# Evacuations of attention projections on VectorE, and the pair projections one head earlier

## The reference

```python
# x: (8, 2048, 1024); layer 0: latent attention, causal, 16 heads, clip, 64 + 32 rope columns
c_q = x @ W_DQ;  Qc = c_q @ W_UQ;  Qr = rope(c_q @ W_QR)
c_kv = x @ W_DKV; Kc = c_kv @ W_UK; Kr = rope(x @ W_KR); V = c_kv @ W_UV
attn = softmax(where(causal, clip(Q @ K.T, -80, 80), -inf) / sqrt(96)) @ V
# layer 1: plain attention, 16 heads of 64, no mask used
q = (x @ q_w.T + q_b) / 8;  k = x @ k_w.T + k_b;  v = x @ v_w.T + v_b
attn = softmax(q @ k.T) @ v
# each block: x = x + layernorm(block(layernorm(x)))
```

## Time and profile before

| What | us |
|---|---|
| Median of 2 runs | 5481.67 (5463.56 and 5499.78) |
| Profiled run | 5459.5 |
| Its span, slowest core | 5457.9 |
| Spans of the eight cores | 5430.5 to 5457.9 |
| PE busy | 3475.7 (64%) |
| DVE busy | 1663.3 (30%) |
| ACT busy | 1806.0 (33%) |

### The profile page before, as it was taken

How to read it: one execution, slowest core, us unless ns; L and a number is a source line. 1 busy time by engine, 2 the same in 40 slices (tenths; PEclk the granted TensorE clock), 3 DMA queues, 4 the chain that set the end, 5 groups by cost and what they waited for, 6 DMA issues and landing times.

```text
span 5457.9 us, 48911 instructions; the slowest of 8 cores (5430.5 to 5457.9 us)
## 1 busy us (share of the span) xinstructions
PE 3475.7 (64%) x10539; PEld 1024.8 (19%) x10539; DVE 1663.3 (30%) x2197; ACT 1806.0 (33%) x2222; POOL 194.1 (4%) x272
## 2 busy tenths in 40 slices
PE   2566666665446666656687687777775466566664
PEld 1111111111112222221111111111111112121211
DVE  3344445455722433321111211211214624010101
ACT  2144444442233221134444444444442320212120
POOL 0000000000000011100000000000000000000000
PEclk9666666666668888875555555555556698989897
DMA  3000000001047332231101101001000056121213
GB/s 77 13 5 5 4 5 4 4 5 19 1 138 219 103 103 93 85 78 31 29 0 29 27 2 29 20 10 29 8 18 18 27 163 197 54 70 54 70 54 116
DMA packets 132278, 275.24 MB, mean 50 GB/s; under 512 B 25731, under 2 KB 60979, under 8 KB 132022
## 3 DMA queue, kind: packets, MB, share of 16 engines
q0 software_dynamic: 62208, 154.22, 10.5%
q10 hardware_dynamic: 45840, 75.51, 4.1%
q1 hardware_dynamic: 23974, 42.38, 2.6%
HBM read 237.02 MB, written 41.94 MB: 51 GB/s over the span
## 4 chain that ended last, share of the span: by engine, by line
PE 45%; DVE 19%; DMA 13%; ACT 11%; issue 10%; DVEq 1%; ACTq 1%; POOLq 0%; SPq 0%; POOL 0%
PE psB L511 11%; PE ps_up L1000 8%; PE psA L461 7%; DVE rrow L523 7%; PE psB L531 4%; ACT pbuf L480 4%; PE ps_dn L1023 3%; PE psB L461 3%; PE ps_dn L1623 2%; DMA w2q_scr<-w2b 2%; DMA w2b<-w2q_scr 2%; DMA wdnq_scr<-w2b 2%; DMA w2b<-wdnq_scr 2%; ACT sqd L1620 2%; ACT hbuf L1610 1%
## 5 line engine op out<-in xcount | busy, mean ns | idle before, releaser
L511 PE MATMUL psB<-pbuf,v_km 128*65 128x512 bf16 (+3 forms) x1664 | 787.6, 564 | 254.1 <-ACT pbuf L480 165.1
L523 DVE RECIPROCAL rrow<-psB 1x512 f32<-1x512 f32 x128 | 429.0, 3352 | 1182.6 <-PE psB L511 1179.4
L480 ACT ACTIVATE pbuf<-psA,negb 128x1024 bf16<-128x1024 f32 x368 | 408.5, 1114 | 445.9 <-PE psB L511 350.9
L1023 PE MATMUL ps_dn<-w2b,hbuf 128*128 128x512 bf16 x1536 | 400.8, 400 | 131.8 <-DMA w2b<-w2q_scr 35.5
L531 PE MATMUL psB<-rrow,c_ones_f 1*64 1x512 f32 x256 | 221.5, 962 | 319.7 <-DVE rrow L523 311.3
L461 PE MATMUL psA<-qpair,kpair 64*128 64x512 bf16 x736 | 375.9, 617 | 28.0 <-ACT pbuf L480 24.3
L480 ACT ACTIVATE pbuf<-psA,nb 128x1024 bf16<-128x1024 f32 (+7 forms) x288 | 255.1, 895 | 357.8 <-PE psB L511 263.4
L1000 PE MATMUL ps_up<-xqT,w1b 128*128 128x512 bf16 x1024 | 250.6, 409 | 171.8 <-DVE hscr L1159 91.5
L511 PEld LDWEIGHTS psB<-pbuf,v_km 128*65 128x65 bf16 x1664 | 170.5, 141 | 835.9 <-issue 832.0
L1623 PE MATMUL ps_dn<-sqd,c_ones_cf 128*1 128x512 f32 x256 | 134.3, 606 | 296.4 <-ACT sqd L1620 296.4
L1000 PE MATMUL ps_up<-xnT,w1b 128*128 128x512 bf16 x1024 | 258.8, 398 | 28.7 <-DVE w1b L1058 21.5
(11 more groups left out here) (257 smaller groups left out, 3462.7 us busy)
## 6 DMA issues: line engine op xcount, KB each, us to landing
w1b<-w1q_scr POOLq DMA_DIRECT2D x24, 1024.0 KB, 6.5
w2b<-w2q_scr POOLq DMA_DIRECT2D x48, 512.0 KB, 4.0
w1b<-wupq_scr POOLq DMA_DIRECT2D x24, 1024.0 KB, 5.8
w2b<-wdnq_scr POOLq DMA_DIRECT2D x48, 512.0 KB, 3.9
al_wf<-wupt ACTq DMA_DIRECT2D x64, 256.0 KB, 2.8
al_wf<-wdnt ACTq DMA_DIRECT2D x64, 256.0 KB, 2.9
xs<-x SPq DMA_DIRECT2D x1, 8192.0 KB
wqf<-w1t SPq DMA_DIRECT2D x8, 1024.0 KB
```

Of the source, the lines that this page charges most:

```text
L480: P.op("scalar", lambda e, sc_ap=sc_ap, pb=pb, kw=kw: e.activation(pb, sc_ap, AF.Exp, **kw), reads=pres, sreads=sr, writes=(pbres,))
L511: q_start=q_start, lastkc=lastkc: e.matmul(psB[:, gq:gq + nn][0:65, :], v_km[:, kc * (H * 65) + h * 65: kc * (H * 65) + h * 65 + 65], pb[: ...
L523: P.op("vector", lambda e, b=b: e.reciprocal(rrow[:], psB[64:65, b * 512:(b + 1) * 512]), reads=(bres,), writes=("rrow",))
L1023: hx=hx, dnp=dnp: e.matmul(dnp[:, n2 * 512:(n2 + 1) * 512], hbuf[:, hc * 512 + qc * 128: hc * 512 + qc * 128 + 128], w2band[bs][:, hx * D ...
```

## The change

Four edits. In layer 0 the six projection evacuations of a head become a `tensor_copy` on DVE. In layer 1 the four evacuations of a pair become a `tensor_scalar` on DVE (multiply, then add the bias), and the two squares of the bounds a `tensor_tensor` on DVE. And the items for pair j+1 ride on the first head of pair j instead of the second, with the bounds directly behind that head. The alpha pieces and the weight loads stay ahead of each pair.

```diff
             def post(slot, half=half):
                 pst, sbase, pres = slot
-                P.op("scalar", lambda e, pst=pst, sbase=sbase, half=half:
-                     e.activation(dst_fn(half),
-                                  pst[:, sbase:sbase + 1024][0:rows, :],
-                                  AF.Identity),
+                P.op("vector", lambda e, pst=pst, sbase=sbase, half=half:
+                     e.tensor_copy(dst_fn(half),
+                                   pst[:, sbase:sbase + 1024][0:rows, :]),
                      reads=pres, writes=(dres,))
...
-                P.op("scalar", lambda e, pst=pst, sbase=sbase, half=half:
-                     e.activation(dst[:, half * 1024:(half + 1) * 1024],
-                                  pst[:, sbase:sbase + 1024], AF.Identity,
-                                  scale=sc, bias=bias[:, j:j + 1]),
+                P.op("vector", lambda e, pst=pst, sbase=sbase, half=half:
+                     e.tensor_scalar(dst[:, half * 1024:(half + 1) * 1024],
+                                     pst[:, sbase:sbase + 1024], sc,
+                                     bias[:, j:j + 1], ALU.mult, ALU.add),
                      reads=pres, sreads=(bres,), writes=(dres,))
...
-            P.op("scalar", lambda e, srcp=srcp:
-                 e.activation(bsq[:], srcp[:], AF.Square),
+            P.op("vector", lambda e, srcp=srcp:
+                 e.tensor_tensor(bsq[:], srcp[:], srcp[:], ALU.mult),
                  reads=(sres,), writes=BSQR)
...
-            extra = pair_prod_items(j + 1) if (hh == 1 and j + 1 < 8) else ()
+            extra = pair_prod_items(j + 1) if (hh == 0 and j + 1 < 8) else ()
             emit_attention_head(
...
-        if j + 1 < 8:
-            pair_bounds(j + 1)
+            if hh == 0 and j + 1 < 8:
+                pair_bounds(j + 1)
```

## The result

| | us |
|---|---|
| Before, median of 10 runs | 5489.3 |
| After, median of 12 runs | 5553.1 |
| Ratio | 1.0112, 95% interval 1.0075 to 1.0150 |
| Profiled runs, span of the slowest core | 5457.9 before, 5532.5 after |

What follows compares the result with a forecast made beforehand. DVE's chain was taken to bound layer-0 head ends; in layer 1, ACT's alpha pieces and the bounds chain counted. 112 + 3 - 24.5 + 18 = 108.5, say 109 us, on 5474 gave 5583 us (+1.99%), range 5530 to 5640.

Steps and rivals of the forecast that it cites:

- the forecast's own +85 to +130: Whole kernel, main case: slower by +85 to +130 us, chance 0.66.
- the first rival: Layer-0 head ends hide more of the evacuations: +40 to +85 us, about 5535; chance 0.12.
- DVE's chain in layer 0: Layer-0 head ends: evacuations in DVE's queue delay the next scores by 7.5 us, 15 x 7.5 = 112 us.
- its own sign of being wrong: The forecast called itself wrong if, among other signs, the layer-0 ends grow by under 6 us.
- The second miss: Layer-0 head end, first broadcast matmul behind 3.4 us of idle PE: taken at 1.93 us, not 1.04.
- The +3 for the projections ahead of the first heads: The 8 + 4 projections ahead of the first heads are serial too: +3 us, bounds 0 to 5.
- The hidden evacuation: Layer-0 head end: last evacuation, behind the last rope step, hidden by the DMA; without that cover it costs 1.2 us.
- Layer 1: Layer-1 head ends: -24.5 us from both ends, +18 from pair loads, gain 6.5 us; bounds -37 to +22.
- Long end: Layer-1 head end with projections and bounds, last exp to next exp: 52.6 us before, 38.4 forecast.
- short end: Layer-1 head end without projections, now with the alpha pieces: 14.5 us before, 25.2 forecast, +3 where pair loads fall.
- The price of the pair loads: Layer-1 short ends: pair loads among the alpha pieces cost +3 us in six ends, +18; bounds 0 and 7 an end.
- The clock's rival: Layer-1 heads keep TensorE's 2.4 GHz level behind the long end: sum -31 us, 5443; chance 0.04.

Runs made afterwards that it cites:

- the kernel with the early loads: Layer 0 of before, layer 1 of after, weight loads of a pair emitted one head earlier; 0.9969 (0.9956 to 0.9981) against the kernel before.
- the run with layer 0 alone: Kernel before with only the six projection evacuations of a layer-0 head on DVE; 1.0136 (1.0113 to 1.0160), 74 us.
- With the loads moved away: Layer 0 of before, layer 1 of after, weight loads two pairs ahead behind a POOL wait on negb; 0.9943 (0.9922 to 0.9965) against before.

## Why the prediction was right or wrong

It gave 5583 us, 109 above its base of 5474, and the range 5530 to 5640. The measured medians are 64 us apart, the ratio says 61, and 5553 lies in the range. That is in part luck. The difference of 61 us does not lie in the forecast's own +85 to +130, which had 0.66, but in the case of the first rival, +40 to +85, which had 0.12; and the measured median of before is 15 us above the base. Within 2% had 0.46, and slower by over 2%, which did not happen, 0.51. The order of the queues and the waits came as told. Two durations taken from one head end were too long, and one effect was not in the sum.

*DVE's chain in layer 0 (+7.5 a head, 112 us): right in kind, nearly a quarter too large.* Measured are 6.1 us a head on the slowest cores, 5.9 on the mean of all, and 90.8 us for the stage. That is at the edge of its own sign of being wrong, under 6 us. By its steps, on the slowest cores: the first reciprocal was to start 4.1 us late, it was 3.4 (3.1 over all cores); between the reciprocals 0.95 was forecast, 0.56 measured; behind them 2.5 and 2.24.

The largest miss is the first. The head that I had read had a slow second projection (1.89 us, 488.52), and the sum took that for every head. In before it takes over 1.6 us in 48 of the 120 head ends of all cores, in after in 11; on the slowest core of after it takes 1.04 to 1.22 us in 11 of 15. Since the reciprocal now stands behind it, it starts that much sooner. This could have been read from the other head ends of before.

The second miss could not. It is the step "After 3.4 us of idle PE I take it at the duration of the one behind 2.9 us of idleness": of 15 first broadcasts ten took 1.04 to 1.2 us and five 1.8 to 1.94, all behind 3.0 to 3.8 us of idle PE; over all cores 57 of 120 were slow. In before all 120 first broadcasts, behind at most 1.2 us of idle PE, were fast, and 119 of the 120 second ones slow, so more head ends would have said the same as the one. The row of the slow kind in after, and the windows around it and around the fast one at 729.38 (PEclk is the number behind ACT's and POOL's busy times):

```profile
656.16 1.93 PE L531 MATMUL psB<-rrow,c_ones_f 1*64 1x512 f32 x2 [3.44 <-DVE rrow L523]
...
656.10:658.10 2.00, 1.94 (x3) 0.36 (x4) 0.00 (x0) 0.00 (x0) 0.00 (x0) 0.50 0.00 0
729.30:730.50 1.20, 1.12 (x3) 0.30 (x4) 0.00 (x0) 0.00 (x0) 0.00 (x0) 0.99 0.00 0
```

The slow one ran at 0.50, the 1.2 GHz level, behind 3.44 us of idle PE; the fast one at 0.99, the 2.4 GHz level, behind 3.76. The idle time ahead of a matmul doesn't tell its clock. The price of this miss is smaller than it looks, because the head that I had read also had 6.65 us between its reciprocals in before, where the mean is 6.31.

One reading was inexact without changing the sum: DVE's work after 494.33 is not "gapless", as the text against the first rival has it. Behind the second reciprocal it waits for the broadcast. The fourth evacuation stands behind that gap in DVE's order and can't use it. In before:

```profile
499.94 0.68 DVE L544 TENSOR_TENSOR astage<-scrA,psB 64x512 bf16<-64x512 bf16 x1 [2.25 <-PE psB L531]
```

The +3 for the projections ahead of the first heads came to 2.0 us in layer 0 (17.3 and 19.3 us from the first projection to the first exp, over all cores) and 0.7 in layer 1.

*The hidden evacuation: right.* The last one costs nothing, shown by its own run; that it even gains 0.4 us was not forecast.

*Layer 1: right in mechanism and in size.* The forecast was -6.5 us, and the stage is 9.8 shorter, of which up to 7 can be scatter. Long end forecast 38.4, measured 38.3 on the slowest core and 38.5 over all; short end 25.2 without and 28.2 with loads, measured 24.1 and 28.7, over all cores 24.6 and 27.6. The square was put at 1.19 us and takes 1.21; the slow ones-matmuls (1.86 in all four) came, too. The evacuation with scale and bias takes 1.28, not 1.23:

```profile
L1337 DVE TENSOR_SCALAR kpair<-psA,kbp 128x1024 bf16<-128x1024 f32 x9 | 11.6, 1283 | 22.6 <-PE psA L1326 22.6
...
L1361 DVE TENSOR_TENSOR pbuf<-qpair 128x2048 bf16<-128x2048 bf16 x8 | 9.7, 1207 | 0.0
```

The Trainium skill's 1224 ns for the square (VectorE: DVE Perf Modes, "The perf-mode tier table") agrees with the 1207 of the row within 2%. In the short end the trace has no table load between exp and Abs, nor behind the pieces. That agrees with the Trainium skill (ScalarE: Activation LUTs, "Table sets: the hidden batching unit"), which has abs in every table set. The price of the pair loads was right in size: +3 forecast, 3.0 between the ends with and without loads over all cores, and 2.1 given back when they were taken from among the pieces.

*The clock's rival didn't happen.* The heads of layer 1 stay at 1.2 GHz behind the new long end (window of 70 us; PEclk is the number behind ACT's and POOL's busy times):

```profile
2705.00:2775.00 70.00, 62.43 (x124) 10.06 (x124) 8.06 (x4) 35.31 (x34) 0.00 (x0) 0.50 0.00 1
```

*Not in the sum: the other stages.* The sum of the two stages is +81, and the ratio says +61, with an interval from +41 to +82. In both kernels with all six evacuations on DVE the untouched stages were 11 us shorter in the profile than in that of before. But so they were in the kernel with the early loads, whose layer 0 is that of before. Over all fourteen profiles the untouched stages range from 2551 to 2571 us, in no order that follows the edits, and within one profile the eight cores differ by 17 to 67 us. The ratios have scatter of this size as well: in the run with layer 0 alone the medians are 84 us apart, while the ratio gives 74. Nothing here shows that a longer layer 0 shortens what follows; to exclude it would take many profiles of the same kernel.

## What to carry to other kernels

At the seams of a pipelined loop, write down each engine's queue in order and ask what stands directly ahead of the step that leads; shares of busy time (ACT 33%, DVE 30%) pointed the other way. Work that belongs to nothing nearby, such as the alpha pieces, is worth most where the paced engine isn't the one that does it: inside the heads it cost 0.5 us a head, at the seams 10 to 23 us an end. And when the price of a step depends on TensorE's clock, read it over all its repetitions before taking the value of one; where the change gives a matmul an idle time that it never had before, as the first broadcast here, carry both durations in the bounds.

## What the runs showed of the hardware that I had not expected

- A broadcast matmul behind 3.0 to 3.8 us of idle PE ran at either clock level: of 120 in the kernel after 57 were slow (about 1.9 us), the others took 1.04 to 1.2 us on the slowest core (rows above).
- An evacuation of 64x1024 from PSUM takes 1.005 to 1.017 us on ACT and 1.204 to 1.216 on DVE; on 32 partitions 1.013 and 1.208. Between 32 and 64 partitions there is no difference on either; a copy of 128x1024 on DVE takes 1.226.
- On the slowest core of after, in each of the six short ends with pair loads among the alpha pieces the longest wait of a piece behind them is 2.6 to 4.0 us; in the seventh, without loads, it is 1.6. With the loads moved away it is still 1.7 to 2.9, with only the astage DMA there.
